# Cross stage of a decoder block: which queue issues the rows of maxima, and in which slots the weight pieces are prepared

## The chip, the cores and the metric

The kernel runs on one core of one Trainium2 chip. The metric is the device time of one execution in microseconds, as a median of several executions; the profile comes from one further execution.
## The reference

Sixteen sequences of 128 rows by 512 columns pass through three layers, each behind a layer norm and each with a residual addition:

- attention with 16 query heads, one key and value head, rotary positions and a causal mask;
- a "cross" layer: attention with 8 heads of 16 channels over 512 positions, in which a position sees those at most 64 away. Its score is softmax(q·k/4), its result is projected, passed through relu, multiplied by a second input `ctx`, and projected once more;
- a feed-forward layer whose two weight matrices are rounded to -1, 0 or 1 after scaling by their mean size, and whose activations are rounded to 8 bits.

The softmax of the cross layer is computed with the true row maximum taken off. The rounding of the feed-forward weights needs a mean over the whole matrix, an offset with a big constant that rounds (w·s + 1.5·2^23), the subtraction of that constant, and a clip to -1..1.

## The kernel before

Three stages follow one another: attention, cross, feed-forward. Everything changed lies in `cross`. It runs a loop over b = -3 .. 18 in every engine's list, and each step b works on several sequences at different points of their way: the maxima of sequence b+1, the exponentials of b, the products with the values of b-1, the output projection of b-2, and so on. A step is divided into 8 slots s = 0 .. 7 on TensorE, VectorE and ScalarE. A slot covers one pair of heads and one half of the positions.

In each slot TensorE computes scores twice. `maximum_scores` writes queries by keys into the PSUM tile `Sm`, of which VectorE takes the negated row maxima (`maxima`, L1292). `shifted_scores` writes keys by queries into the PSUM tile `Se`; here the operand `Q` has three more rows, which hold the negated maxima split in three bf16 parts, so that the matmul takes the maximum off. ScalarE takes the exponentials of it (`exponentials`, L1130). There is one `Sm` and one `Se`: the next `Sm` waits for the maxima of this one, and the next `Se` waits for the exponentials of this one. In TensorE's list a slot is: `Sm` of slot s, `Se` of slot s, then the other products of the slot (values in slots 0 to 2, output projection in 2, value projection in 3, query and key projection in 5 and 6, the last projection in 7).

The maxima are turned by TensorE into `Bb` (`maxima_turned`, slot 0 for the second half and slot 4 for the first half of the next sequence), split by ScalarE (`maxima_high`), VectorE (`maxima_rest`) and GpSimd (`maxima_low`) into the tile `m3`, and then written by three DMAs of 4 KB into the rows of `Q` (`maxima_rows`). Half 1 of sequence b is needed by `Se` in slot 4 of step b; half 0 of sequence b+1 by `Se` in slot 0 of the next step.

SyncE issues all DMAs of the stage in one list. Per step: the load of `ctx`; the spreading of the query parts from DRAM to `Q` (3 DMAs, 768 KB); the keeping of the key parts to DRAM (384 KB); the rows of maxima of half 1; the spreading of the key parts (4 DMAs, 768 KB); the rows of half 0; the keeping of the query parts (384 KB); and a weight piece (704 KB).

The feed-forward weights come in 12 pieces (`PIECES`) over two staging buffers `w_stage`. A piece n is offset by VectorE (`offset`, L1316), has the constant taken off by ScalarE (L1181) and is clipped by VectorE (`clip`, L1322). In step b VectorE offsets piece b in slot 1, behind the maxima of slot 1; ScalarE converts piece b at the end of slot 2, behind the exponentials of that slot; VectorE clips piece b-1 in slot 2. In slot 3 ScalarE copies the values' product out of PSUM (`oU`, L1154) ahead of its exponentials, and VectorE shuffles that copy (L1347) behind its maxima.

Of the kernel before, what the change touches and what calls it, by code (L numbers as in the profile page):

```python
# [10 lines left out]
ACT = mybir.ActivationFunctionType  # L11
# [4 lines left out]
D = 512  # L16
# [29 lines left out]
PIECES = [(0, i * F, (i + 1) * F) for i in range(2 * KD)] + [(1, a * D, min(a + 3, KF) * D) for a in range(0, KF, 3)]  # L46
# [814 lines left out]
XH = 8  # L861
XD = P // XH
BAND = 64
TS = 64
# [8 lines left out]
ROWS = len(Q_PARTS) * XD  # L873
# [74 lines left out]
def real(b):  # L948

    return not isinstance(b, int) or 0 <= b < B  # L950

def cross(nc, t, dram):

    with ExitStack() as ctx:
        def sb(name, shape, dt):
            return ctx.enter_context(nc.sbuf_tensor(f"x_{name}", shape, dt))

        def sem(name):
            return ctx.enter_context(nc.semaphore(f"x_{name}"))  # L960
# [8 lines left out]
        Q, K, Vw, mx = t["Q"], t["K"], t["Vw"], t["mx"]  # L969
# [3 lines left out]
        m3 = [sb(f"m3{i}", [32, 3, TS], BF16) for i in range(2)]  # L973
# [3 lines left out]
        w_stage = [sb(f"w_stage{i}", [P, WIDEST], F32) for i in range(2)]  # L977
# [11 lines left out]
        m_high, m_rest, m_mid, m_low = sem("m_high"), sem("m_rest"), sem("m_mid"), sem("m_low")  # L989
        m_in = [sem(f"m_in{i}") for i in range(2)]  # L990
# [6 lines left out]
        w_rounded, w_whole, k_ones = sem("w_rounded"), sem("w_whole"), sem("k_ones")  # L997
# [5 lines left out]
        def wait(eng, signal, count):  # L1003

            if count > 0:
                eng.wait_ge(signal, count)

        def steps(step):

            for b in range(-3, B + 3):  # L1010
                step(b)
# [109 lines left out]
        @block.scalar  # L1121
        def _(act):
            act.preload_act_table_set("natural_log_exp_and_others")

            def exponentials(b, s):
                p, hf = divmod(s, 2)
                wait(act, se_full, SLOTS * b + s + 1)
                if s == 4:
                    wait(act, pv_full, b)
                act.activation(ex[:, (PAIRS * b + p) % RING, 4 * hf * WIN:4 * (hf + 1) * WIN].rearrange("p (j c) -> p j c", j=2),  # L1130
                               Se[:, :, 0:2 * WIN], ACT.Exp, scale=XD ** -0.5).then_inc(ex_ready, 1)

            def maxima_high(b, half):
                wait(act, t_full, 2 * b + half + 1)
                wait(act, m_in[half], M_IN * b)
                act.activation(m3[half][:, 0, :], Bb[0:32, 0:TS], ACT.Copy).then_inc(m_high, 1)

            def high(dst, half, b, full, kept, ready):
                wait(act, full, b + 1)
                wait(act, kept, 16 * b)  # L1140
                act.activation(dst[:, 0, :], XY[:, half, :], ACT.Identity, bias=t["bqk"][:, half:half + 1]).then_inc(ready, 1)

            def middle(dst, rest, b, rest_ready, ready):
                wait(act, rest_ready, b + 1)
                act.activation(dst[:, 1, :], rest[:, :], ACT.Copy).then_inc(ready, 1)

            def step(b):
                for s in range(SLOTS):
                    if s == 1 and real(b):
                        maxima_high(b, 1)  # L1150
                    if s == 3 and real(b - 1):
                        wait(act, pv_full, b)
                        wait(act, oN_ready, b - 1)
                        act.activation(oU[:, :, :], XY[:, :, :], ACT.Copy).then_inc(o_ready, 1)  # L1154
                    if s == 4 and real(b - 2):
                        wait(act, out_full, b - 1)
                        wait(act, wct_full, b - 2)
                        act.activation(gate[:, :], Bb[:, :], ACT.Relu, bias=t["bo"][:, 0:1]).then_inc(gate_ready, 1)
                    if s == 5 and real(b + 1):
                        maxima_high(b + 1, 0)  # L1160
                    if s == 6 and real(b + 3):
                        high(qp, 0, b + 3, q_full, q_kept, q_high)
                    if s == 7 and real(b + 3):
                        high(kp, 1, b + 3, k_full, k_kept, k_high)
                        middle(qp, qr, b + 3, q_rest, q_mid)
                    if real(b):
                        exponentials(b, s)
                    if s == 0 and real(b + 2):
                        middle(kp, kr, b + 2, k_rest, k_mid)
                    if s == 4 and real(b - 1):  # L1170
                        wait(act, sums_ready, b)
                        act.activation(rl[:, :, :], rl[:, :, :], ACT.Ln).then_inc(ln_ready, 1)
                    if s == 5 and real(b - 1):
                        wait(act, ln_ready, b)
                        for hh in range(2):
                            act.activation(rl[:, hh, :], rl[:, hh, :], ACT.Exp, scale=-1.0,
                                           bias=t["live"][:, hh:hh + 1]).then_inc(rl_ready, 1)
                    if s == 2 and 0 <= b < len(PIECES):
                        i, lo, hi = PIECES[b]
                        wait(act, w_rounded, b + 1)  # L1180
                        act.activation((t["gateQ"], t["downQ"])[i][:, lo:hi], w_stage[b % 2][:, 0:hi - lo], ACT.Copy,  # L1181
                                       bias=-MAGIC).then_inc(w_whole, 1)

            steps(step)

        @block.gpsimd
# [41 lines left out]
        @block.sync  # L1228
        def _(sp):
            def keep(name, src, b, done_sem, read, runs, kept):  # L1230

                wait(sp, read, runs * b)
                wait(sp, done_sem, b + 1)
                sp.dma_start(parts[name].rearrange("j p t -> p j t"), src[:, :, :]).then_inc(kept, 16)

            def spread(name, tiles, runs, b, kept, landed):

                wait(sp, kept, 16 * (b + 1))
                wait(sp, se_full, SLOTS * (b - 2))
                for to, first, n in runs:  # L1240
                    sp.dma_start(tiles[b % 3][to * XD:(to + n) * XD, :, :].rearrange("r h t -> r (h t)"),
                                 parts[name][first:first + n].rearrange("j (d h) t -> (j d) (h t)", d=XD)).then_inc(landed, 16)

            def maxima_rows(b, half):

                wait(sp, m_low, 2 * b + half + 1)
                for k in range(3):
                    to = bass.AP(Q[b % 3], (ROWS + k) * XH * D + half * 4 * D, [[XH * D, 1], [TS, 32], [1, TS]])
                    sp.dma_start(to, m3[half][:, k, :]).then_inc(m_in[half], 16)

            def step(b):
                if real(b - 2):
                    wait(sp, y_ready, b - 2)
                    sp.dma_start(ctxb[:, :], dram["ctx"][b - 2]).then_inc(ctx_in, 16)
                if real(b + 2):
                    spread("q", Q, Q_RUNS, b + 2, q_kept, q_in)
                    keep("k", kp, b + 2, k_low, k_in, K_IN, k_kept)
                if real(b):
                    maxima_rows(b, 1)
                if real(b + 2):  # L1260
                    spread("k", K, K_RUNS, b + 2, k_kept, k_in)
                if real(b + 1):
                    maxima_rows(b + 1, 0)
                if real(b + 3):
                    keep("q", qp, b + 3, q_low, q_in, Q_IN, q_kept)
                if 0 <= b + 1 < len(PIECES):
                    wait(sp, w_whole, b)
                    load_piece(sp, dram, b + 1, w_stage[(b + 1) % 2]).then_inc(w_in[(b + 1) % 2], 16)

            steps(step)  # L1270

        @block.vector
        def _(dve):
# [44 lines left out]
            def clip(n):  # L1318
                i, lo, hi = PIECES[n]
                piece = (t["gateQ"], t["downQ"])[i][:, lo:hi]  # L1320
                wait(dve, w_whole, n + 1)
                dve.tensor_scalar(piece, piece, 1.0, -1.0, ALU.min, ALU.max)  # L1322
# [5 lines left out]
            def step(b):  # L1328
# [4 lines left out]
                for s in range(SLOTS):  # L1333
# [23 lines left out]
                        rest(qp, qr, 0, b + 3, q_high, q_low, q_rest)  # L1357
                    if s == 7 and real(b + 3):
                        rest(kp, kr, 1, b + 3, k_high, k_low, k_rest)
                    if s == 1 and 0 <= b < len(PIECES):  # L1360
                        offset(b)
                    if s == 2 and 0 <= b - 1 < len(PIECES):
                        clip(b - 1)
                    if b >= B - 1 and s % 2 == 1:

                        first = (b - B + 1) * 4 + s // 2
# [489 lines left out]
```

## Time and profile before

| what | us |
|---|---|
| median of 3 executions | 1238.08 (1236.08 to 1243.37) |
| profiled execution, its own time | 1235.82 |
| profiled execution, span from first to last instruction | 1234.0 |
| cross stage, first `Sm` to last exponentials | 653 to 1001 |
| engines busy over the span: PE, DVE, ACT, POOL | 1035.4, 813.1, 647.5, 640.5 |

The span lies 1.8 us below the time of the same execution. In what follows, "a step" runs from one `Sm` of slot 0 to the next one, and times are from the start of the span. The first whole step of the pipeline starts at 671.66; twelve steps, which are those in which a weight piece is offset, end at 928.38. Two more steps without an offset follow.

### The profile page before, as it was taken

What the parts mean: (1) busy time and instruction counts of PE and PEld (TensorE: products, weight loads), DVE (VectorE), ACT (ScalarE), POOL (GpSimd) and SP (SyncE); (2) the same over time, 40 slices, a digit from 0 to 9 for tenths busy, and PEclk for the clock granted to TensorE, in tenths of its full rate; (3) what the DMA queues carried; (4) which work ended last, traced back from release to release, by engine and by line L of the source; (5) the groups of instructions that cost most, each with busy time, mean ns of one, the idle gap of its engine ahead of it and who ended that gap; (6) DMA issues with size and microseconds to landing.
All of it is one profiled execution on the core that took longest, in us unless ns stands there. A gap on an engine that the chain in (4) does not pass through costs nothing. (4 is left out here: it accounts for less than half of the span.)

```text
span 1234.0 us, 25423 instructions
## 1 busy us (share of the span) xinstructions
PE 1035.4 (84%) x9604; PEld 774.9 (63%) x9604; DVE 813.1 (66%) x1487; ACT 647.5 (52%) x1188; POOL 640.5 (52%) x584
## 2 busy tenths in 40 slices
PE   5689999999999999999635888989899954777675
PEld 5578887888888888887413666656566631333332
DVE  7678776666666666576334667676666645888884
ACT  5555545455454545556512566666556542455553
POOL 3665666566565657566315143434334334566653
PEclk9899999999999999999867899999999976899998
DMA  9043643233233332346336666665755200000000
GB/s 348 21 172 122 246 166 120 110 138 136 81 131 133 136 113 97 133 160 211 134 75 153 149 168 164 168 160 135 187 130 135 60 19 32 18 17 25 25 25 27
DMA packets 51135, 147.57 MB, mean 120 GB/s; under 512 B 10448, under 2 KB 24272, under 8 KB 39760
## 3 DMA queue, kind: packets, MB, share of 16 engines
q1 hardware_dynamic: 42288, 86.93, 25.3%
q0 software_dynamic: 8064, 58.72, 13.0%
q8 instruction: 75, 1.23, 0.4%
q10 hardware_dynamic: 672, 0.40, 0.1%
q14 instruction: 36, 0.29, 0.1%
HBM read 120.46 MB, written 25.17 MB: 118 GB/s over the span
## 5 line engine op out<-in xcount | busy, mean ns | idle before, releaser
L1292 DVE TENSOR_REDUCE mx<-Sm 128x4 f32<-128x768 f32 x128 | 122.4, 956 | 87.7 <-PE Sm L1032 87.2
L1130 ACT ACTIVATE x_ex<-Se 128x768 f32<-128x768 f32 x128 | 103.1, 805 | 116.4 <-PE Se L1032 116.0
L282 PE MATMUL Qb<-a_xTh,WqH 128*128 128x256 f32 x512 | 146.3, 286 | 3.1 <-DVE a_vl L800 3.0
L283 PE MATMUL Qb<-a_xTl,WqH 128*128 128x256 f32 x512 | 145.6, 284 | 0.0
L284 PE MATMUL Qb<-a_xTh,WqL 128*128 128x256 f32 x512 | 145.4, 284 | 0.0
L627 POOL TENSOR_TENSOR a_pr<-a_pr_plain,a_ph 128x512 fp32r<-128x512 f32 x64 | 83.6, 1307 | 110.2 <-ACT a_ph L447 110.0
L740 DVE TENSOR_TENSOR a_turned<-Qb,sinS 64x512 f32<-64x512 f32 (+1 forms) x144 | 94.9, 659 | 62.6 <-PE Qb L284 45.1
L609 POOL TENSOR_TENSOR a_ql<-a_rot,a_qh 128x512 fp32r<-128x512 f32 x64 | 83.9, 1315 | 98.4 <-ACT a_qh L467 98.2
L459 ACT ACTIVATE Lb<-Lb 128x512 f32<-128x512 f32 x64 | 37.2, 582 | 170.4 <-PE Ob L354 170.4
L367 PE MATMUL Yb<-a_WoH,a_oH 128*128 128x512 f32 x256 | 103.2, 403 | 5.5 <-POOL a_oN L605 5.5
L282 PEld LDWEIGHTS Qb<-a_xTh,WqH 128*128 128x128 f32 x512 | 98.6, 193 | 6.9 <-issue 2.4
L369 PE MATMUL Yb<-a_WoH,a_oN 128*128 128x512 f32 x256 | 101.3, 396 | 0.0
L368 PE MATMUL Yb<-a_WoL,a_oH 128*128 128x512 f32 x256 | 101.1, 395 | 0.0
L283 PEld LDWEIGHTS Qb<-a_xTl,WqH 128*128 128x128 f32 x512 | 98.6, 193 | 2.4
L284 PEld LDWEIGHTS Qb<-a_xTh,WqL 128*128 128x128 f32 x512 | 98.6, 193 | 0.0
L605 POOL TENSOR_TENSOR a_oN<-a_oN_plain,a_oH 128x512 fp32r<-128x512 f32 x64 | 84.9, 1327 | 3.0 <-ACT a_oH L439 3.0
L1024 PE MATMUL Sm<-band,ident_b 128*64 128x256 bf16 x512 | 54.9, 296 | 31.2 <-DVE mx L1292 18.2
L756 DVE TRANSPOSE_TENSOR_REDUCE a_rmax<-Sb 128x16 f32<-128x512 f32 x64 | 45.6, 712 | 51.6 <-PE Sb L334 51.5
L1024 PEld LDWEIGHTS Sm<-band,ident_b 128*64 128x64 bf16 x512 | 19.0, 111 | 90.3 <-issue 46.1
L636 POOL TENSOR_TENSOR Dg<-ident,a_negm 32x512 fp32r<-32x512 f32 x64 | 66.5, 1039 | 13.2 <-DVE a_negm L763 10.5
L1578 POOL TENSOR_TENSOR f_hg<-f_h,g 128x512 f32<-128x512 f32 (+1 forms) x48 | 56.0, 1181 | 32.3 <-DVE f_h L1658 32.3
L1482 PE MATMUL Gb<-gateQ,f_xqT 128*128 128x512 bf16 (+1 forms) x192 | 48.0, 374 | 29.1 <-DVE f_h L1658 27.4
(202 smaller groups left out, 2841.4 us busy)
## 6 DMA issues: line engine op xcount, KB each, us to landing
a_WoH<-wo_parts POOLq DMA_DIRECT2D x28, 1024.0 KB, 5.2
a_WoL<-wo_parts POOLq DMA_DIRECT2D x28, 1024.0 KB, 7.2
K<-k_parts SPq DMA_DIRECT2D x32, 256.0 KB, 4.8
q_parts<-x_qp SPq DMA_DIRECT2D x16, 384.0 KB, 3.0
Q<-q_parts SPq DMA_DIRECT2D x16, 384.0 KB, 5.6
k_parts<-x_kp SPq DMA_DIRECT2D x16, 384.0 KB, 7.4
a_w_stage<-in_gateT SPq DMA_DIRECT2D x8, 704.0 KB, 4.5
x_w_stage<-in_gateT SPq DMA_DIRECT2D x8, 704.0 KB, 5.1
```

Of the source, the lines that this page charges most:

```text
L282: pe.matmul(out, w_hi(k), xTh[:, k, :], start=(k == 0), stop=False)
L283: pe.matmul(out, w_hi(k), xTl[:, k, :], start=False, stop=False)
L284: mm = pe.matmul(out, w_lo(k), xTh[:, k, :], start=False, stop=(k == KD - 1))
L367: pe.matmul(Yb[s % 2][:, :], high, WoH[u % 2][:, i, :], start=(i == 0), stop=False)
L368: pe.matmul(Yb[s % 2][:, :], high, WoL[u % 2][:, i, :], start=False, stop=False)
L369: mm = pe.matmul(Yb[s % 2][:, :], low, WoH[u % 2][:, i, :], start=False, stop=(i == HG - 1))
L605: pool.tensor_tensor(oL[:, s % 2, :], oN[:, s % 2, :], oH[:, s % 2, :].bitcast(F32), ALU.subtract).then_inc(oL_ready, 1)
L609: pool.tensor_tensor(rot_dst(False, True, par, r), rbuf(par, r)[:, 0:rot_width(r)], rot_dst(True, False, par, r).bitcast(F32), ALU.subtrac ...
L627: pool.tensor_tensor(pl[:, :], pr[:, :], ph[:, :].bitcast(F32), ALU.subtract).then_inc(pl_ready, 1)
L740: dve.tensor_tensor(dst[to:to + hi - lo, 0:width].rearrange("p (j c) -> p j c", c=P), bank[lo:hi, 0:width].rearrange("p (j c) -> p j c", c=P),
L1130: act.activation(ex[:, (PAIRS * b + p) % RING, 4 * hf * WIN:4 * (hf + 1) * WIN].rearrange("p (j c) -> p j c", j=2), Se[:, :, 0:2 * WIN], A ...
L1292: dve.tensor_reduce(mx[:, half, at:at + 4].rearrange("p (j a) -> p j a", j=2), Sm[:, :, 0:2 * WIN].rearrange("p j (a c) -> p j a c", a=2), ...
```

## The change

The rows of maxima are no longer issued by SyncE. ScalarE issues them: half 1 of sequence b in slot 2 of step b, right behind the exponentials of slot 2, and half 0 of sequence b+1 in slot 6, right behind the exponentials of slot 6. The waits and the DMAs themselves are the same. The offset of piece b moves on VectorE from slot 1 to slot 3, where it stands behind the maxima and the shuffles and ahead of the maxima of slot 4. ScalarE converts piece b-1 in slot 2 of step b instead of piece b, and VectorE clips piece b-2 instead of b-1.

```diff
@@ scalar @@
+            def maxima_rows(b, half):
+
+                wait(act, m_low, 2 * b + half + 1)
+                for k in range(3):
+                    to = bass.AP(Q[b % 3], (ROWS + k) * XH * D + half * 4 * D, [[XH * D, 1], [TS, 32], [1, TS]])
+                    act.dma_start(to, m3[half][:, k, :]).then_inc(m_in[half], 16)
...
                     if real(b):
                         exponentials(b, s)
+                    if s == 2 and real(b):
+                        maxima_rows(b, 1)
+                    if s == 6 and real(b + 1):
+                        maxima_rows(b + 1, 0)
...
-                    if s == 2 and 0 <= b < len(PIECES):
-                        i, lo, hi = PIECES[b]
-                        wait(act, w_rounded, b + 1)
-                        act.activation((t["gateQ"], t["downQ"])[i][:, lo:hi], w_stage[b % 2][:, 0:hi - lo], ACT.Copy,
+                    n = b - 1
+                    if s == 2 and 0 <= n < len(PIECES):
+                        i, lo, hi = PIECES[n]
+                        wait(act, w_rounded, n + 1)
+                        act.activation((t["gateQ"], t["downQ"])[i][:, lo:hi], w_stage[n % 2][:, 0:hi - lo], ACT.Copy,
                                        bias=-MAGIC).then_inc(w_whole, 1)
@@ sync @@
-            def maxima_rows(b, half):
-                wait(sp, m_low, 2 * b + half + 1)
-                for k in range(3):
-                    ...
-                    sp.dma_start(to, m3[half][:, k, :]).then_inc(m_in[half], 16)
...
-                if real(b):
-                    maxima_rows(b, 1)
                 if real(b + 2):
                     spread("k", K, K_RUNS, b + 2, k_kept, k_in)
-                if real(b + 1):
-                    maxima_rows(b + 1, 0)
@@ vector @@
-                    if s == 1 and 0 <= b < len(PIECES):
+                    if s == 3 and 0 <= b < len(PIECES):
                         offset(b)
-                    if s == 2 and 0 <= b - 1 < len(PIECES):
-                        clip(b - 1)
+                    if s == 2 and 0 <= b - 2 < len(PIECES):
+                        clip(b - 2)
```

## Rows read from the trace of the kernel before

**Rows 1.** Table by stretch: span, busy of each engine, granted clock, DMA share, GB/s.
```profile
796.14:817.23 21.09, 18.84 (x346) 12.91 (x345) 14.68 (x25) 13.49 (x20) 8.20 (x10) 1.00 0.67 163
928.38:947.51 19.13, 18.78 (x345) 12.90 (x344) 13.73 (x24) 12.30 (x19) 8.28 (x10) 1.00 0.62 141
947.51:967.35 19.84, 18.07 (x341) 13.35 (x340) 11.68 (x20) 10.80 (x16) 7.90 (x10) 0.91 0.59 137
671.66:928.38 256.72, 226.91 (x3994) 156.65 (x3994) 172.90 (x281) 158.72 (x234) 93.00 (x104) 0.97 0.65 158
```

**Rows 2.** Waits of TensorE from 655 to 1000: us in total, times, longest.
```profile
PE Sm L1024 <- DVE mx L1292: 18.2, 17, 3.5
PE Se L1024 <- DMA Q<-x_m: 10.2, 10, 2.1
```

**Rows 3.** The staging tile of the weight pieces: its offset, DVE's wait, time to landing.
```profile
L1316 DVE TENSOR_SCALAR x_w_stage<-x_w_stage,w_inv x12: 753/953/1020, 678.4 to 910.7; 128x1408 f32<-128x1408 f32 x8, 128x1536 f32<-128x1536 f32 x3, 128x1024 f32<-128x1024 f32 x1
...
  DVE x_w_stage L1316: 25.7, 12
...
DMA to landing us min/median/max: 4.6/5.1/7.8
```

**Rows 4.** Timeline of the step from 796.14, slots 1 to 3: start, duration, engine.
```profile
804.29 0.95 DVE L1316 TENSOR_SCALAR x_w_stage<-x_w_stage,w_inv 128x1408 f32<-128x1408 f32 x1 [3.66 <-DMA x_w_stage<-in_gateT]
805.16 0.95 DVE L1292 TENSOR_REDUCE mx<-Sm 128x4 f32<-128x768 f32 x1
...
805.27 1.38 ACT L1181 ACTIVATE gateQ<-x_w_stage 128x1408 bf16<-128x1408 f32 x1 [2.08 <-DVE x_w_stage L1316]
...
806.16 0.41 PE L1024 MATMUL Sm<-band,ident_b 128*64 128x256 bf16 x4 [2.06 <-DVE mx L1292]
```

**Rows 5.** The rows of maxima: duration of an issue, time to landing, then one half 1.
```profile
L1249 SPq DMA_DIRECT2D Q<-x_m x96: 503/592/1877, 669.7 to 989.7; - x96
...
DMA to landing us min/median/max: 1.6/2.5/7.2
...
760.38 3.07 SPq L1249 DMA_DIRECT2D Q<-x_m  x3
...
767.62 0.41 PE L1024 MATMUL Se<-band,ident_b 128*64 128x256 bf16 x4 [1.10 <-DMA Q<-x_m]
```

**Rows 6.** Timeline of the step from 928.38, slots 2 to 5, by engine.
```profile
934.85 0.81 ACT L1130 ACTIVATE x_ex<-Se 128x768 f32<-128x768 f32 x1 [1.49 <-PE Se L1032]
935.62 1.02 ACT L1154 ACTIVATE x_oU<-XY 128x1024 f32<-128x1024 f32 x1
...
938.14 0.72 DVE L1347 STREAM_SHUFFLE x_rl<-x_oU 128x512 f32<-128x512 f32 x1
...
939.51 0.96 DVE L1292 TENSOR_REDUCE mx<-Sm 128x4 f32<-128x768 f32 x1
...
940.52 0.41 PE L1024 MATMUL Sm<-band,ident_b 128*64 128x256 bf16 x4
```

**Rows 7.** Timeline of slots 6 to 0 around 755: exponentials of 6 and 7, next `Se`.
```profile
752.33 0.78 ACT L1130 ACTIVATE x_ex<-Se 128x768 f32<-128x768 f32 x1
753.02 0.66 ACT L1141 ACTIVATE x_kp<-XY,bqk 128x512 bf16<-128x512 f32 x1
...
754.16 0.81 ACT L1130 ACTIVATE x_ex<-Se 128x768 f32<-128x768 f32 x1
...
756.09 0.41 PE L1024 MATMUL Se<-band,ident_b 128*64 128x256 bf16 x4
```

**Rows 8.** Start of the program: an issue on ScalarE's queue beside ScalarE's work.
```profile
0.74 1.28 ACT L398 ACT_TABLE_LOAD   x1 [0.74 <-PEq L1845]
...
0.84 0.47 ACTq L402 DMA_DIRECT2D gamma<-in_gamma  x1
```

**Rows 9.** The spreading of the keys: its issue on SyncE, its landing.
```profile
787.70 1.75 SPq L1241 DMA_DIRECT2D K<-k_parts  x4
...
K<-k_parts SPq DMA_DIRECT2D x30, 256.0 KB, 4.8
```

More of the change, by code:

```diff
@@ L1242, in spread @@
                                  parts[name][first:first + n].rearrange("j (d h) t -> (j d) (h t)", d=XD)).then_inc(landed, 16)
-            def maxima_rows(b, half):
-                wait(sp, m_low, 2 * b + half + 1)
-                for k in range(3):
-                    to = bass.AP(Q[b % 3], (ROWS + k) * XH * D + half * 4 * D, [[XH * D, 1], [TS, 32], [1, TS]])
-                    sp.dma_start(to, m3[half][:, k, :]).then_inc(m_in[half], 16)
             def step(b):
```

## The prediction

> **What bounds the kernel now.** I read the table by stretch first. The twelve steps in which a weight piece is offset take 256.72 us, 21.39 each, and TensorE is busy for 226.91 of them, 18.9 per step; the step behind them, which offsets nothing, takes 19.13 with TensorE busy for 18.78, and the next one 19.84 [rows 1]. So the stage stands at TensorE's own work once nothing disturbs it, and a piece costs about 2.2 us of idle TensorE per step. The view of waits says for whom it idles: 18.2 us for VectorE's maxima and 10.2 us for the rows of maxima [rows 2]. The third view, the staging tile, shows why the maxima are late: VectorE sits idle for 25.7 us in front of the 12 offsets, 2.1 us each, until the piece lands [rows 3]. In the step from 796.14 it stands for 3.66 us, the maxima of slot 2 start at 805.16 behind the offset, and TensorE has waited 2.06 us when it starts the next `Sm` [rows 4]. The fourth view, the rows' own tile, shows that the other wait is a landing and not an issue: half 1 is issued by 763.45, and `Se` waits until 767.62, with 1.10 us of TensorE idle, while the shortest time from issue to landing is 1.6 [rows 5]. Both waits stand on the path that sets the end of the stage, since TensorE has nothing else to do in them.
>
> **The change, part by part.** The rows come from one execution of 1235.82 us, 2.3 below the median of 1238.08; I work out a difference and apply it to both.
>
> *Offset to slot 3.* In slot 1 the wait on the piece goes away. A piece lands at most 7.8 us after its issue [rows 3], and slot 3 begins about 8 us into a step, behind the shuffles at about 10 us [rows 6], so the offset itself finds the piece there. The duration of 0.95 us does not go away. It now stands between the shuffles and the maxima of slot 4. In the step without an offset the shuffles begin at 938.14, the maxima at 939.51, and the next `Sm` at 940.52 follows their end at 940.47 directly [rows 6]: slot 4 has no cover on VectorE, and every 0.1 us there is TensorE's.
>
> *Rows of half 1 and the conversion, slot 2 of ScalarE.* Without a piece the exponentials of slot 2 start 6.47 us into the step (934.85 less 928.38) and the copy oU follows at 7.24 [rows 6]. Now three issues stand between. One takes 0.59 us [rows 5], three 1.78. Do they begin when the exponentials end or when they begin? At the start of the program an issue on ScalarE's queue begins at 0.84, in the middle of a table load that runs from 0.74 to 2.02 [rows 8]. So I take it that the queue issues while the engine computes. The next activation then starts 6.5 + 1.8 = 8.3 us into the step. The conversion takes 1.38 [rows 4], to 9.7; it waits for no one, as its piece was offset a step earlier. oU takes 1.02 [rows 6], with a little overlap to 10.65. The shuffles of VectorE wait for oU and take 1.37 (938.14 to 939.51), to 12.05; the offset 0.95, to 13.0; the maxima of slot 4 0.96, to 13.9; `Sm` of slot 5 starts at 13.95. In the step without a piece it started at 940.52 - 928.38 = 12.14. So this chain costs 1.8 us, of which some 0.2 come back in slot 5, where that step waits for the maxima and the new one doesn't: a step with offset and conversion takes 19.13 + 1.8 - 0.2 = 20.75 us.
>
> *What the rows of half 1 gain.* Issued 6.5 to 8.3 us into the step, they land, at 1.6 to 2.5 us from issue [rows 5], by 10.3, against 11.4 at which `Se` of slot 4 asks for them. The 10.2 us of waits [rows 2] go, but not on top of the above: they lay in the same slots 4 that the chain now fills, so they are in the difference between 21.39 and 20.75.
>
> A rule of the skill speaks against this part. The Trainium skill, DMA: Bandwidth & Descriptors, section Issuing engines are not separate DMA queues, says that DMAs of all issuers run on the same 16 engines and interleave, and that a second issuer saves only issue time. By that alone half 1 would go on landing 4 to 5 us after its last issue, as the row of 760.38 does, at some 13 us, just before `Sm` of slot 5: it would leave the sum within 0.2 us per step. The same page's section Queues, rings and completion order says that an engine takes turns between queues packet by packet, by which the rows would no longer stand behind the 1.1 MB issued on SyncE just ahead. No row here shows the rows on a second queue.
>
> *Rows of half 0, slot 6.* The exponentials of slot 6 start at 752.33, and the key copy follows at 753.02. With three issues from 752.35 it starts at 754.15, 1.1 us later, and so do the exponentials of slot 7: they end at 756.07 instead of 754.97. The `Se` that waits for them starts at 756.09 [rows 7]. The cover is used to the last tenth, and I cost this at 0. The rows land 1.6 us after the last issue begins, at 755.2. Without the overlap the delay is 1.8 and the cost 0.7.
>
> *SyncE and the keys.* SyncE loses six issues a step and gains nothing to wait for. But the copies behind slot 6's issues feed the keeping of the queries, behind which all bulk transfers of the step stand, so these start about 1 us later in the step. The keys are issued from 787.70 on, over 1.75 us, and land 4.8 us after an issue: by 794.2, or 1.9 before the `Sm` at 796.14 that needs them [rows 9, 1]. One us is covered. GpSimd is busy for 8.2 us a step [rows 1] and stays so.
>
> *Sum.* Eleven steps offset and convert: 11 x 20.75 = 228.2. The first of the twelve only offsets and has no shuffles: some 20. Together 248.3 against 256.7, 8.4 less. The step from 928.38 now converts a piece without an offset: +0.9 (the chain of 1.8 less 0.95). The one from 947.51 (19.84) has neither and loses its wait on rows, at the 19.0 of its neighbour: -0.8. Total -8.4 us: 1227.4 for the profiled execution and 1229.7 as a median.
>
> **Bounds of the unknown.** No row shows three issues behind one activation on ScalarE. From below: an issue takes 0.47, as on ScalarE's queue at 0.84 [rows 8], three 1.4: 0.4 less in each of eleven steps, and with shorter stalls fewer falls of the clock (0.97 over the twelve steps, 1.00 in the steps without long waits [rows 1]): to about -16. From above: three issues take 3.07, as on SyncE behind bulk [rows 5], or begin only when the exponentials end. I take 1.78 with overlap, the median row.
>
> **Rivals.**
> 1. *The issues hold ScalarE in full, and the stage gets slower.* If an issue begins only when the activation ahead has ended, each half costs ScalarE 1.8 us. Slot 4 gets 0.8 more, slot 7's exponentials come 0.7 behind TensorE: 20.75 + 1.5 = 22.25, times 11 against 21.39 is +9.5 us, +1.5 in the two steps behind, and 1 less in the first: +10, 1248. It speaks for it that ScalarE has no gap between slots 6 and 7 [rows 7]; against it stands the overlap [rows 8]. It decides once the step exceeds 21.39, that is from 0.65 us more than I take.
> 2. *No change.* The issues overlap but take 2.3 to 3.1 for three instead of 1.78 [rows 5], half of it on the path: +0.5 to +0.8 per step, which eats the 8.4. Time 1237. For it: the rows were slower to issue just when bulk had been issued ahead.
> 3. *More gain.* Issues of 0.47, or a shuffle chain that starts earlier since slots 0 to 2 are no longer disturbed, and a clock that stays up: 1222. The clock was granted at 0.91 in the stretch from 947.51, which is a part of it at 1.2 GHz [rows 1]; it fell after long idle stretches of TensorE, and the change takes the longest away.
>
> **How the numbers follow.** Forecast 0.45, rival 1 0.2, rival 2 0.2, rival 3 0.15. This kernel's measurement can't tell less than 0.5% (6.2 us) from no change. Faster: most of the forecast's 0.45 and all of rival 3, less what falls short of 6.2, and a little of rival 2: 0.5. Same: 0.27. Slower: rival 1 with the tail of 2, 0.23. The forecast's own range is 1225 to 1234; the range of 8 in 10 goes from 1220 (rival 3) to 1247 (all but the tail of rival 1).
>
> **What would show it.** The offset's wait of 25.7 us gone to under 2. Slot 2 at 2.9 us throughout, and slot 4 at 3.5 to 3.8 in the eleven steps, ended by VectorE's maxima. Wait of `Se` for the rows under 2 us in total. ScalarE's key copy 1.8 us behind the start of slot 6's exponentials; if it is 2.5 or more, rival 1. The prediction is wrong if the steps aren't near 20.75, or if TensorE waits for rows or keys in them.

## The result and the profile after

The changed kernel takes 1259.43 us (median of 4, 1254.18 to 1261.38) against 1240.72 for the kernel before in the same runs: a ratio of 1.0145, 95% interval 1.0092 to 1.0197. It is slower, by 1.4%. The forecast was 1229.7, in a range of 1220 to 1247.

The table by stretch of the kernel after, columns as in [rows 1]: the twelve steps in which a piece is offset, then three neighbouring steps.

```profile
671.63:948.24 276.61, 241.70 (x3992) 165.39 (x3993) 172.48 (x280) 161.16 (x235) 100.25 (x103) 0.90 0.60 146
...
785.99:809.23 23.24, 20.16 (x347) 13.80 (x346) 14.71 (x25) 13.81 (x21) 9.09 (x9) 0.93 0.59 147
809.23:830.39 21.16, 18.72 (x345) 12.91 (x344) 14.08 (x24) 13.02 (x20) 9.06 (x9) 1.00 0.64 162
830.39:854.98 24.59, 21.73 (x345) 14.48 (x344) 15.20 (x25) 14.86 (x23) 9.47 (x10) 0.86 0.56 139
```

The twelve steps grew from 256.72 to 276.61 us, by 19.9 of the 22.9 us between the two spans. Read the first two numbers against each other: TensorE's busy time for the same matmuls grew from 226.91 to 241.70, by 14.8, with the granted clock down from 0.97 to 0.90, and its idle time from 29.8 to 34.9, by 5.1. So only a quarter of the loss is further waiting. The three single steps show the other part: the step at clock 1.00 takes 21.16, its neighbour at 0.86 takes 24.59 for the same 345 matmul records, 3.0 of the 3.4 us between them as busy time.

The waits of TensorE in the same twelve steps: total, times, longest. First the kernel before ([rows 2] reach from 655 to 1000, over more steps), then the kernel after.

```profile
PE Sm L1024 <- DVE mx L1292: 13.2, 9, 3.5
PE Se L1024 <- DMA Q<-x_m: 8.6, 8, 2.1
```

```profile
PE Se L1024 <- DMA Q<-x_m: 15.9, 11, 3.3
PE Bb L1054 <- ACT x_gate L1165: 13.2, 9, 2.8
PE Sm L1024 <- DVE mx L1293: 4.6, 7, 1.1
```

The wait for the maxima fell from 13.2 to 4.6 us, as foreseen, and the one for the rows rose from 8.6 to 15.9. The wait of `Bb` for the gate is new. One step of the kernel after, from 809.23, slots 2 to 5, from the timelines of SP, ACT, DVE and PE:

```profile
814.82 1.35 SPq L1253 DMA_DIRECT2D Q<-q_parts  x3
816.27 1.25 SPq L1246 DMA_DIRECT2D k_parts<-x_kp  x1
...
815.47 0.81 ACT L1130 ACTIVATE x_ex<-Se 128x768 f32<-128x768 f32 x1 [1.50 <-PE Se L1032]
815.48 2.70 ACTq L1143 DMA_DIRECT2D Q<-x_m  x3
818.23 1.38 ACT L1193 ACTIVATE gateQ<-x_w_stage 128x1408 bf16<-128x1408 f32 x1 [1.94 <-issue]
819.51 1.01 ACT L1161 ACTIVATE x_oU<-XY 128x1024 f32<-128x1024 f32 x1
820.41 0.80 ACT L1130 ACTIVATE x_ex<-Se 128x768 f32<-128x768 f32 x1
821.10 0.69 ACT L1165 ACTIVATE x_gate<-Bb,bo 128x512 f32<-128x512 f32 x1
...
820.56 0.72 DVE L1348 STREAM_SHUFFLE x_rl<-x_oU 128x512 f32<-128x512 f32 x1
...
821.80 0.94 DVE L1317 TENSOR_SCALAR x_w_stage<-x_w_stage,w_inv 128x1408 f32<-128x1408 f32 x1
822.65 0.95 DVE L1293 TENSOR_REDUCE mx<-Sm 128x4 f32<-128x768 f32 x1
...
821.85 0.30 PE L1054 MATMUL Bb<-ident,mx 128*32 128x64 f32 x2 [1.75 <-ACT x_gate L1165]
...
822.38 0.41 PE L1024 MATMUL Se<-band,ident_b 128*64 128x256 bf16 x4
...
823.66 0.41 PE L1024 MATMUL Sm<-band,ident_b 128*64 128x256 bf16 x4 [0.56 <-DVE mx L1293]
```

Three things end slot 4 within 2 us of each other. The gate ends at 821.79, and TensorE's turning of the maxima has waited for it, because both use `Bb`. The rows land at 822.33, and `Se` starts at 822.38. The maxima stand behind shuffles and offset until 823.6. That is 14.4 us into the step; with no piece it was 12.14 (940.52 less 928.38) [rows 1, 6].

What such an idle stretch of TensorE is followed by shows one step earlier. Note the first matmuls of the next `Sm`, which had 0.41 us each time above:

```profile
798.71 0.30 PE L1054 MATMUL Bb<-ident,mx 128*32 128x64 f32 x2 [1.85 <-ACT x_gate L1165]
...
800.35 0.41 PE L1024 MATMUL Se<-band,ident_b 128*64 128x256 bf16 x4 [1.23 <-DMA Q<-x_m]
...
800.90 0.59 PE L1024 MATMUL Sm<-band,ident_b 128*64 128x256 bf16 x4
```

Slot 5 of this step and slot 5 of the next one in the table by stretch; the granted clock stands third from the end:

```profile
800.90:804.77 3.87, 3.87 (x30) 2.17 (x26) 2.87 (x7) 3.39 (x6) 0.41 (x2) 0.56 0.84 203
823.66:825.94 2.28, 2.28 (x26) 1.34 (x27) 2.22 (x5) 2.28 (x5) 0.20 (x1) 1.00 1.05 180
```

TensorE was idle for over 3 us in two pieces, and then most of slot 5 ran at the lower of its two levels (1.2 instead of 2.4 GHz): 3.87 us instead of the 2.28 of the next step, which kept its clock. In the changed kernel slot 5 stands at a granted clock of 0.50 to 0.69 in eleven of the twelve steps, behind a slot 4 with 1.8 to 3.3 us of idle. In the kernel before it does so in one, the one whose slot 4 had its longest idle (2.14 us). But the idle of slot 4 alone doesn't decide it: the step that kept its clock had 2.44 us of it.

### The profile page after: what moved, and what is told of

Same layout as the page of the kernel before. It is cut to its first block and busy times, and to the rows that moved or that the text cites. A ratio compares the mean times of both kernels' runs of the same rounds, so it can differ in the third digit from the quotient of the medians.

```text
span 1256.9 us, 25423 instructions
## 1 busy us (share of the span) xinstructions
PE 1052.7 (84%) x9604; PEld 785.9 (63%) x9604; DVE 813.2 (65%) x1487; ACT 649.9 (52%) x1188; POOL 647.8 (52%) x584
## 5 line engine op out<-in xcount | busy, mean ns | idle before, releaser
L1225 POOL TENSOR_TENSOR x_gate<-x_gate,x_ctxb 128x512 f32<-128x512 f32 x16 | 27.5, 1717 | 104.5 <-ACT x_gate L1165 104.5
L1024 PE MATMUL Se<-band,ident_b 128*64 128x256 bf16 x512 | 55.2, 298 | 24.4 <-DMA Q<-x_m 16.9
L636 POOL TENSOR_TENSOR Dg<-ident,a_negm 32x512 fp32r<-32x512 f32 x64 | 66.5, 1039 | 13.2 <-DVE a_negm L763 10.5
L1024 PEld LDWEIGHTS Sm<-band,ident_b 128*64 128x64 bf16 x512 | 19.9, 113 | 85.1 <-issue 60.3
```

The source lines that it names most:

```text
L1024: pe.matmul(at, t["ident_b"][:, TS * hh:TS * hh + TS], masks, start=True, stop=True, skip_group_check=True)
```

## The experiments

The numbers of the twelve steps come from each kernel's table by stretch and view of waits; slot lengths are the mean distances of `Sm` starts in them. Each kernel has one trace, while medians are over several runs; where the two disagree the text says so. Each ratio is to runs of the kernel before made alongside, whose median lay between 1236.69 and 1241.47 us, so kernels are to be compared by ratios rather than by times.

| kernel | ratio to before (95%) | 12 steps | PE busy | clock | idle | slot 2 | slot 4 | slot 5 |
|---|---|---|---|---|---|---|---|---|
| before | 1 | 256.7 | 226.9 | 0.97 | 29.8 | 4.19 | 2.44 | 2.83 |
| changed | 1.0145 (1.0092, 1.0197) | 276.6 | 241.7 | 0.90 | 34.9 | 2.85 | 4.42 | 3.84 |
| e1 rows only | 1.0134 (1.0095, 1.0173) | 274.8 | 231.4 | 0.94 | 43.4 | 4.93 | 2.67 | 2.89 |
| e2 pieces only | 1.0087 (1.0048, 1.0125) | 264.8 | 232.3 | 0.94 | 32.5 | 3.20 | 3.73 | 3.24 |
| e6 pieces a step later | 1.0046 (1.0023, 1.0070) | 261.5 | 230.2 | 0.95 | 31.3 | 3.31 | 3.37 | 3.29 |
| e3 slot 4 filled | 1.0146 (1.0087, 1.0204) | 272.0 | 243.0 | 0.95 | 29.0 | 2.75 | 4.44 | 3.44 |
| e5 conversion in slot 1 | 1.0134 (1.0084, 1.0184) | 268.7 | 231.9 | 0.94 | 36.8 | 2.88 | 3.87 | 3.49 |
| e9 spread after rows | 1.0126 (1.0092, 1.0161) | 269.6 | 229.7 | 0.96 | 39.9 | 2.86 | 3.37 | 2.71 |
| e7 rows first | 0.9959 (0.9936, 0.9983) | 261.5 | 229.9 | 0.96 | 31.6 | 3.55 | 1.82 | 2.51 |
| e8 rows first, pieces later | 1.0016 (0.9986, 1.0045) | 255.7 | 227.0 | 0.97 | 28.7 | 3.17 | 1.82 | 2.53 |
| e10 keep, rows, spread; pieces later | 0.9839 (0.9813, 0.9866) | 241.8 | 222.8 | 0.99 | 19.0 | 3.43 | 1.83 | 2.57 |
| e11 keep, rows, spread; old pieces | 0.9808 (0.9778, 0.9839) | 240.3 | 224.5 | 0.98 | 15.7 | 3.59 | 1.85 | 2.54 |
| e12 as e10, load earlier | 1.0024 (0.9993, 1.0054) | 266.1 | 229.9 | 0.95 | 36.1 | 2.74 | 1.88 | 2.55 |
| e14 as e11, changed pieces | 0.9918 (0.9886, 0.9949) | 250.1 | 225.9 | 0.97 | 24.2 | 3.01 | 3.09 | 2.75 |

### Each half of the change alone

**e1**: the scalar and sync hunks of the rows, pieces as before.

```diff
+ act: if s == 2: maxima_rows(b, 1);  if s == 6: maxima_rows(b + 1, 0)
- sp:  maxima_rows(b, 1);  maxima_rows(b + 1, 0)
```

> The rows of maxima issued by ScalarE, the weight pieces in their old slots. Theory (the chain on ScalarE): the three issues push conversion, oU, exponentials and gate of slots 3 and 4 back; TensorE's turning of the maxima in slot 4 waits for the gate, Se for the rows. But the maxima of slot 4 don't stand behind an offset. Steps of 21.4 to 22.3, that is 0 to 10 us over the kernel before (1240 to 1251), the waits of TensorE split between slot 2 (offset, about 2 us) and slot 4 (gate and rows, 1 to 2 us), fewer low-clock stretches than in the changed kernel. Rival (the rows' own queue is the whole loss, the pieces' move is neutral): as slow as the changed kernel, 1255 to 1262. Rows land 4 us or more after the last issue in both.

Measured 1255.28 (1.0134). It is at the rival's time, but most of the waiting of the twelve steps is not in slot 4: `Sm` waits for VectorE's maxima, in slot 2 (4.93).

```profile
PE Sm L1024 <- DVE mx L1292: 28.1, 17, 4.9
PE Se L1024 <- ACT x_ex L1130: 5.7, 12, 1.2
PE Se L1024 <- DMA Q<-x_m: 5.5, 6, 1.6
PE Bb L1054 <- ACT x_gate L1165: 3.5, 4, 1.2
```

VectorE waited 42.0 us for pieces instead of 25.7 [rows 3]; the view of the staging tile says:

```profile
  DVE x_w_stage L1316: 42.0, 12
```

So issuing the rows from ScalarE alone costs about as much as the whole change. Its trace shows SyncE's bulk (the large transfers) coming later: the keeping of the queries is issued 1.75 us into a step on average instead of 0.50, and the pieces land at 8.2 instead of 6.6. The changed kernel has the same delay (1.44, and 7.5). That this delay is all that e1 loses by I have not isolated.

**e2**: the hunks of the pieces alone, rows by SyncE as before.

```diff
- dve: s == 1: offset(b);   s == 2: clip(b - 1);   act: s == 2: convert b
+ dve: s == 3: offset(b);   s == 2: clip(b - 2);   act: s == 2: convert b - 1
```

> The pieces in their new slots, the rows issued by SyncE as before. Theory: slot 2 at 2.9 us, no wait for a piece; the conversion starts at 7.3 us into a step, gate done by 11; slot 4 at 3.3 to 3.6 us, set by the rows' landing and by the offset in front of the maxima of slot 4; steps of 20.8, 1232 to 1236. Rival (the offset in front of the maxima of slot 4 is the loss): slot 4 over 4 us and a low clock in slot 5, slower than before, 1245 to 1255.

Measured 1247.25 (1.0087), in the rival's range, with a lower clock in slot 5 (3.24 us long) but slot 4 at 3.73, not over 4. The stretch and its first two waits:

```profile
672.02:936.80 264.78, 232.27 (x3993) 160.39 (x3993) 179.26 (x280) 159.07 (x233) 93.15 (x104) 0.94 0.63 153
```

```profile
PE Se L1024 <- DMA Q<-x_m: 20.6, 9, 4.1
PE Sm L1024 <- DVE mx L1293: 6.8, 9, 1.7
```

The wait for the rows more than doubled (from 8.6 in the kernel before) without a change to the rows. The two losses, 0.9% and 1.3%, sum to 2.2%, more than the 1.45% of both together: they overlap.

### The two waits of the kernel before cover each other

**e6**: the offset keeps slot 1 but takes the piece of the step before.

```diff
- dve: s == 1: offset(b);      s == 2: clip(b - 1);   act: s == 2: convert b
+ dve: s == 1: offset(b - 1);  s == 2: clip(b - 2);   act: s == 2: convert b - 1
```

> Rows by SyncE as before; piece b-1 instead of b is offset in slot 1 and converted in slot 2, so that the offset keeps its slot and finds its piece landed. Theory: the wait of 25.7 us goes and nothing is put into slot 4; what is left is the rows' landing in slot 4 (about 1 us a step): steps of 20.0 to 20.5, 1224 to 1232. Rival (the old wait for the piece was covered by the wait for the rows): 1236 to 1241.

Measured 1242.75 (1.0046): the rival's outcome, just above its range. Nothing was added to slot 4 and VectorE no longer waits for pieces, yet TensorE's wait for the rows in the twelve steps is this:

```profile
PE Se L1024 <- DMA Q<-x_m: 20.8, 10, 3.7
```

The rows land 13.1 us into a step on average in both kernels; what sets that time the next experiments ask. Slots 0 to 3 made faster only bring TensorE to `Se` of slot 4 earlier. The idle time moves from slot 2 (14.9 to 4.6 us in twelve steps) to slot 4 (8.4 to 21.0), and the granted clock is 0.95 against 0.97.

### What the rows wait for

**e4**: the changed kernel, SyncE waits for the rows before it keeps the keys.

```diff
+ if real(b): wait(sp, m_in[1], M_IN * (b + 1))
  keep("k", kp, b + 2, k_low, k_in, K_IN, k_kept)
```

> The changed kernel, but SyncE starts the writing of the key parts to DRAM only when the rows of half 1 have landed. Theory A (the rows' completion waits for the key parts' write, which is in flight on the other queue): rows land 1.2 to 1.6 us after the end of their last issue instead of 4 to 5.5. Theory B (they wait for the spreading of the queries or for all bulk): they still land 3 us or more after it. In both the keys come later, so the first product of a step may wait for them and the time says little (1255 to 1290).

Theory B. One run gave 1262.35 (no ratio can be given); its twelve steps took 273.0 us. The view of the rows' tile for single halves, minimum, median and maximum of the three transfers' times from issue to landing: the kernel before at 801.7, the kernel after at 815.5 (half 1) and 827.8 (half 0, with no bulk ahead), and e4 at 795.5.

```profile
DMA to landing us min/median/max: 5.6/5.7/6.4
```

```profile
DMA to landing us min/median/max: 4.8/5.2/5.3
...
DMA to landing us min/median/max: 1.7/1.8/1.8
```

```profile
DMA to landing us min/median/max: 4.7/4.8/5.0
```

In these steps a row takes 5.2 us on ScalarE's queue instead of 5.7 on SyncE's behind bulk, and 1.8 with none. Over all halves 1 of the twelve steps the difference is smaller still: 5.6 us on average (3.9 to 6.6) against 5.7 (4.3 to 7.2). The keys' write is not what holds the rows, since e4 had none in flight; the spreading of the queries, issued from 793.79 on, was in flight. e9 below tests that it is what they wait for.

The packet records of the changed kernel show where the time goes. In slot 6 the first packet of the rows starts 1.2 us after the first issue. In slot 2 it starts 3.0 to 5.5 us after it in eleven of the twelve steps, and in that time 62 to 96 packets of 8 KB start on SyncE's queue, on which the queries are being spread.

**e7**: the kernel before, rows first in SyncE's step.

```diff
+ maxima_rows(b, 1)
+ keep("k", kp, b + 2, ...)
  spread("q", Q, Q_RUNS, b + 2, q_kept, q_in)
- keep("k", kp, b + 2, ...)
- maxima_rows(b, 1)
  spread("k", K, K_RUNS, b + 2, k_kept, k_in)
```

> The kernel before, in which SyncE issues the rows of half 1 first in its step, then keeps the keys, then spreads the queries; pieces in their old slots. Theory (the rows' landing stands behind the 8 KB packets of the spreading of the queries, on any queue): rows land 1.2 to 1.6 us after the last issue, at 8 to 9 us into the step, TensorE's wait for them (10.2 us) is gone, the wait for pieces stays: steps of 20.4 to 20.9, 1227 to 1233. Rival (bulk put behind the rows makes the keys late): a wait for K at the start of steps, 1240 or more.

Measured 1236.06 (0.9959, under what I call a change), between the two. Both sides of the expectation came true: slot 4 at 1.82, and the keys late. Trace and median disagree here: the traced execution, with 261.5 us in the twelve steps against 256.7, took 1242.92 us, the longest of ten.

```profile
PE Sm L1024 <- DMA K<-k_parts: 15.7, 8, 3.3
...
PE Se L1024 <- DMA Q<-x_m: 2.8, 5, 0.7
```

**e8**: e7 and e6 together.

> As e7_rows_first, and piece b-1 instead of b offset in slot 1 and converted in slot 2 (as e6_lag). Theory: both waits covered each other in the kernel before, so each fix alone is worth little and both together free slot 2 and slot 4: steps of 19.1 to 19.6 with the granted clock at 1.00, 1210 to 1220. Rival (something else, instruction fetch or the clock, holds the steps at 21): 1230 to 1240.

Measured 1242.31 (1.0016): no gain, just above the rival's range. (The traced execution, at 1237.65, was one of the shorter ones, so the 255.7 us of its twelve steps flatter it.) The keys are waited for ten times in the twelve steps, 18.3 us in all. A third wait had stood behind the two.

### How much of slot 4 is ScalarE's chain, the clock, the landing

**e5**: the changed kernel, conversion behind the exponentials of slot 1.

```diff
- if s == 2 and 0 <= n < len(PIECES):
+ if s == 1 and 0 <= n < len(PIECES):
```

> The changed kernel with the conversion of a piece behind the exponentials of slot 1, where ScalarE has 1.5 us of idle, instead of behind the issues of slot 2: oU, gate and shuffles come 1.4 us earlier. Theory: TensorE's wait for the gate in slot 4 (14.8 us in all) goes, but the rows land at 13 to 14 us into the step whatever ScalarE does, so the wait for rows grows by most of it; slot 4 at 3.6 to 4.2 instead of 4.4, 3 to 6 us faster than the changed kernel, 1252 to 1257. Rival (the chain through conversion, oU and gate is what sets slot 4): slot 4 at 3.0 to 3.3 and 12 to 18 us faster, 1241 to 1247.

Measured 1254.76 (1.0134). The time is in the theory's range, but against the changed kernel's 1.0145, with overlapping intervals, no gain is shown. The waits moved as the theory has it: in the trace the one for the gate fell from 13.2 to 2.1 and the one for the rows rose from 15.9 to 23.9:

```profile
PE Se L1024 <- DMA Q<-x_m: 23.9, 12, 3.6
...
PE Bb L1054 <- ACT x_gate L1165: 2.1, 4, 1.4
```

**e3**: the changed kernel, `Sm` of slot 4 computed three times.

```diff
+ for _ in range(2 if s == 4 else 0):
+     unit(Sm, ROWS, s, Q[b % 3], K[b % 3])
  unit(Sm, ROWS, s, Q[b % 3], K[b % 3]).then_inc(sm_full, 1)
```

> The changed kernel, in which TensorE computes Sm of slot 4 three times instead of once (same values), in the time in which it otherwise waits for the gate and the rows: 1.3 us more work per step in slot 4, idle there down by as much. Theory (clock): of the 19.9 us by which twelve steps grew, 14.8 are TensorE's same work at a lower granted clock, brought about by the long idle of slot 4; with the idle filled the clock stays near 1.00, slot 5 goes from 3.9 back to 2.8 and the kernel is 8 to 16 us faster than the changed one, 1243 to 1251, though it computes more. Rival (slot 5 is long for another reason, or the clock falls from the stage's average load): 1257 to 1262, granted clock of the twelve steps 0.90 as before.

Measured 1260.38, no gain: the rival's time. In the trace the clock of the twelve steps did rise from 0.90 to 0.95 and slot 5 fell from 3.84 to 3.44, and the twelve steps took 272.0 instead of 276.6; outside them the same execution lost that again. The extra work filled only a third of slot 4's idle (29.9 to 20.3 us). That agrees with the idle of slot 4 having to do with the clock, but does not show that the clock can be had back at a gain. As a test of what the clock costs it is inconclusive.

**e9**: the changed kernel, the spreading of the queries held until the rows have landed.

```diff
+ keep("k", kp, b + 2, k_low, k_in, K_IN, k_kept)
+ if real(b): wait(sp, m_in[1], M_IN * (b + 1))
  spread("q", Q, Q_RUNS, b + 2, q_kept, q_in)
- keep("k", kp, b + 2, k_low, k_in, K_IN, k_kept)
```

> The changed kernel, in which SyncE first keeps the keys, then waits until the rows of half 1 have landed, and only then spreads the queries. ScalarE's lists and the pieces are those of the changed kernel. Theory (two things hold slot 4 of the changed kernel, the chain through ScalarE to the gate and the rows landing behind the spreading of the queries): rows land by 9.5 to 10.5 us into the step, TensorE's wait for them (16 us in twelve steps) goes, the wait for the gate (13 us) stays or grows to 20, slot 4 at 3.4 to 3.9, 5 to 12 us faster than the changed kernel: 1247 to 1254. Rival (the ScalarE chain alone sets slot 4): 1257 to 1261.

Measured 1256.22 (1.0126): between the two in time, and by its ratio not shown to differ from the changed kernel. The first four waits of the twelve steps:

```profile
PE Sm L1024 <- DMA K<-k_parts: 12.0, 7, 4.0
PE Sm L1024 <- DVE mx L1295: 10.9, 14, 1.6
PE Bb L1054 <- ACT x_gate L1165: 8.6, 9, 1.8
PE Se L1024 <- ACT x_ex L1130: 4.9, 6, 1.3
```

For one half 1 of e9, issued at 816.8, the rows' tile says:

```profile
DMA to landing us min/median/max: 2.2/2.3/2.6
```

Over the twelve steps a row of half 1 takes 2.4 us on average (1.7 to 3.7) instead of 5.6, and the rows land 11.0 us into a step instead of 13.6. Queue and issuing engine are those of the changed kernel, so it was the spreading that they stood behind. The wait for the rows fell to 1.6, slot 4 to 3.37 and slot 5 to 2.71, with 0.96 as the clock of the twelve steps. What is left in slot 4 is gate and offset. The keys, made late by the added wait, took back the gain.

### An order in which nothing is late

**e10**: SyncE keeps the keys, issues the rows, then spreads queries and keys; pieces as e6. **e11**: the same order, pieces as in the kernel before.

```diff
+ keep("k", kp, b + 2, ...)
+ maxima_rows(b, 1)
  spread("q", Q, Q_RUNS, b + 2, q_kept, q_in)
- keep("k", kp, b + 2, ...)
- maxima_rows(b, 1)
  spread("k", K, K_RUNS, b + 2, k_kept, k_in)
```

> Rows by SyncE; its order is keep the keys, rows of half 1, spread the queries, spread the keys; piece b-1 offset in slot 1 and converted in slot 2. Theory (with the rows no longer behind the spreading, with the keys written early and with no wait for pieces, nothing is left to wait for): rows landed by 9 us into the step, keys 2 us or more ahead of their use, steps of 19.2 to 20.0, granted clock 0.99 or more: 1212 to 1222. Rival (the bulk transfers bound a step at about 21 us whatever their order, as in e8_rows_first_lag): 1235 to 1242.

> As e10_keep_rows_spread with the pieces in their old slots. Theory: the waits for pieces in slot 2 stay at about 1.5 us a step, slot 4 is at 1.8: steps of 20.2 to 21, 1224 to 1232. Rival (bulk bounds the step): 1235 to 1242.

Measured 1220.72 (0.9839), as the theory has it, and 1217.04 (0.9808): both beat both kernels, the kernel before by 1.6% and 1.9%, and e11 is better than expected, with no change on any other engine. Its stretch and what TensorE still waits for:

```profile
672.70:912.97 240.27, 224.53 (x3993) 155.17 (x3993) 172.92 (x281) 158.25 (x234) 92.99 (x104) 0.98 0.72 168
```

```profile
PE Sm L1024 <- DVE mx L1292: 6.9, 9, 2.9
PE XY L1075 <- issue: 3.0, 3, 1.2
PE Sm L1024 <- DMA K<-k_parts: 2.7, 2, 1.9
...
PE Se L1024 <- DMA Q<-x_m: 0.7, 3, 0.3
```

The DMA share rose from 0.65 to 0.72 since the same bytes pass in less time. With the pieces a step later (e10) the maxima cost only 1.3, but the keys 7.8: the bulk chain is then what a step waits for.

**e12**: e10 with the load of a piece right behind the spreading of the keys.

> As e10_keep_rows_spread, and SyncE loads the next piece right behind the spreading of the keys instead of at the end of its step, so that the keeping of the queries and of the keys has no piece ahead of it. Theory: the same 1212 to 1222, keys still earlier; the rows of half 0 land a little later, still in time. Rival: the piece is in front of the rows of half 0, Se of slot 0 waits for them 1 us or more a step, 1228 to 1240.

Measured 1243.76 (1.0024): the rival's outcome, above its range. The rows of half 0 now stand behind the piece, `Se` waits 21.3 us for rows (with slot 0 at 4.86), and the keys are late besides (10.6).

**e14**: e11 with the pieces in the slots of the change.

> As e11_keep_rows_spread_old_pieces (SyncE: keep the keys, rows of half 1, spread the queries, spread the keys), with the pieces in the slots of the change: offset of piece b in slot 3 ahead of the maxima of slot 4, conversion of piece b-1 in slot 2. The rows no longer land late, so what slot 4 costs here is the offset and the chain through conversion and oU alone. Theory: Sm of slot 5 follows 0.9 us later than without a piece, slot 4 at 2.6 to 2.9 us ended by VectorE's maxima, slot 2 at 2.9 to 3.4: steps of 19.8 to 20.5, 1219 to 1227. Rival (the offset in slot 3 is what made the changed kernel slow): slot 4 at 3.5 or more, low clock in slot 5, 1232 to 1245.

Measured 1227.3 (0.9918), at the top of the theory's range, with slot 4 at 3.09, a little over it:

```profile
669.19:919.28 250.09, 225.88 (x3992) 155.88 (x3992) 177.35 (x280) 159.78 (x233) 93.39 (x104) 0.97 0.68 162
```

```profile
PE Sm L1024 <- DVE mx L1293: 18.2, 14, 1.9
```

With rows on SyncE and on time, offset and conversion in their new places cost 9.8 us in twelve steps over e11, 0.8 a step, most of it in slot 4 (+1.2, less 0.6 in slot 2). So the part of my chain that comes from the pieces alone is real, at about half of the 19.9 us that the change cost in these steps.

## Why the prediction was wrong

*The waits of the kernel before.* Right as read: 25.7 us of VectorE's wait for pieces went to 0.5, slot 2 to 2.85. Wrong was to treat it as time that could be had. e6 shows that the rows' landing stood behind it.

*Three issues beside the exponentials.* The overlap was right: the first issue begins 0.01 us behind the activation. Half 0 took 1.8 us in every step, as taken, and in ten of twelve the key copy followed 1.9 us behind the start of the exponentials; near 827 it was 2.3, because the issue had waited for GpSimd's low part. Costing it at nothing was right: all waits of `Se` for exponentials come to 0.9 us in twelve steps. Half 1 is the term that I sized wrongly: 2.7 us in the step shown, 1.8 to 3.6 over the twelve steps and 2.3 on average, so that the conversion shown began 9.0 us into the step instead of 8.3. SyncE issuing at the same time doesn't explain the long ones: 2.8 us without it, 1.8 beside 1.1 us of it. My 1.78 was the median over both halves; half 1 alone took 2.2 on average on SyncE in the kernel before.

*"They land ... by 10.3."* This step failed first. They landed 12.6 to 14.3 us into the step, 13.6 on average, against 13.1 before. I took the landing times of rows without bulk ahead (1.6 to 2.5) for rows on another queue. I weighed the rule that speaks against it, the Trainium skill, DMA: Bandwidth & Descriptors, section Issuing engines are not separate DMA queues, and priced it at 0.2 us a step because the landing would still be just ahead of `Sm` of slot 5. The measurements agree with that rule (5.6 us on average from ScalarE against 5.7 from SyncE), and the price is what was wrong: `Se` waited 15.9 us for the rows in twelve steps, 1.3 a step. From the rule of taking turns by packets, in the Trainium skill, DMA: Bandwidth & Descriptors, section Queues, rings and completion order, I had drawn that the rows would no longer stand behind the bulk. Here they did: up to 96 packets of 8 KB of SyncE's queue started between their issue and their first packet.

*The chain of slot 4 ran through VectorE only.* The sum followed oU, shuffles, offset, maxima. It left out that ScalarE's gate also stands behind oU and that TensorE turns the next maxima into the bank the gate reads. TensorE's list has the turning ahead of `Se`, so the gate held `Se` too: 13.2 us. No row of the kernel before showed that wait; it is in the code, at L1088 to L1091 (slot 4 of TensorE's step).

*The clock.* In the forecast TensorE's busy time was to stay at 18.9 us a step. I had made falls of the clock a bonus of rival 3, to be lost or not, and never a price. Yet the forecast itself put 1.8 us of new idle into one slot. Against its 248.3 us for the twelve steps, the 276.6 measured are 28.3 more: 14.8 in busy time at the lower clock, and 13.5 in idle. That the lower clock went with the idle of slot 4 stands in eleven of twelve steps of one trace, and in e9 and e14, where slot 4 is shorter and slot 5 back at 2.7. How far the clock's cost could be undone alone stays open (e3).

*SyncE and the keys.* The 1 us of slip was right in size (the queries are kept 1.4 us into a step on average, instead of 0.5), but I looked only at the keys, which stayed 1.5 to 4.9 us early, and not at what else the bulk held: the rows.

*The rivals.* Rival 1 named the sign, at half the size (+10), with a mechanism that did not happen: the issues did not wait for the activation ahead.

What stays open: how much of e1's loss comes from the later pieces, and how much from ScalarE's three issues by themselves. No kernel was run with the rows on ScalarE, the bulk out of their way and the keys on time.

## What to carry to other kernels

Before a wait is taken away, find the transfer or engine that sets the end of the slots behind it: where two waits follow one another on the same engine and the later one ends at a time that the earlier one doesn't move, removing the earlier one only lengthens the later. A small transfer that others wait for was made faster here by what is issued ahead of it, not by which queue issues it: three lines in another order gave 1.9%. And idle time of TensorE can cost more than itself, when the work behind it runs at the lower clock. The changed kernel had 34.9 us of idle, 29.9 of it in slot 4, at a clock of 0.90; e9 had 39.9, 19.4 of it in slot 4, at 0.96. That it is the gathering in one slot that does it is argued from such single traces and not isolated.

## What the runs showed of the hardware

- An issue on ScalarE's queue starts while an activation runs (815.48 beside 815.47) and holds the next one: three took 1.8 us in slot 6, and 1.8 to 3.6 in slot 2 (2.3 on average).
- A 4 KB transfer behind the spreading of the queries (768 KB) landed 4.6 to 6.6 us after its issue from a second queue (changed kernel, halves 1 of eleven steps), 4.3 to 7.2 from the same one (kernel before), and 1.7 to 1.8 with nothing ahead (half 0 at 827.8).
- From the second queue, the first packet of such a transfer started 1.2 us after the issue in slot 6, and 3.0 to 5.5 us after it behind the spreading, in eleven of twelve steps.
- For the same work TensorE was busy for 241.7 us at a mean granted clock of 0.90, 226.9 at 0.97 and 222.8 at 0.99.
